# A decoder block in fp32r: where the attention matrices are transposed, when the cross-attention steps run, a second buffer for Wq's rows, and every second place for the ternary pieces

## The chip, the core and the metric

The kernel runs on one core of one Trainium2 chip. The metric is device time in microseconds (us), lower is better. All times below are of the same inputs.

## What is computed

x and ctx have shape 4 x 512 x 512. Three residual blocks follow each other, each behind a layer norm (LN, eps 1e-5):

```
x = x + attn(LN(x))          # 16 heads of 128; q, k, v = LN(x) @ W + b; softmax; @ Wo + bo
x = x + gamma * xattn(LN(x), ctx)   # 8 heads of 64, softmax over 512, along the sequence axis
x = x + ffn(LN(x))           # silu(x @ w1q.T) * (x @ w3q.T) @ w2q.T, hidden 1365
# w1q, w3q, w2q: ternary: s = mean|w|; clip(round(w / s), -1, 1) * s
```

The attention of a head attends over the 128 features and not over the sequence (q is transposed to 128 x 512, k to 512 x 128), so a score matrix is 128 x 128 per head and batch, and it can be had from the Gram matrix G = LN(x)^T LN(x) of a batch.

## The kernel before, in words

All products are made of fp32r pieces: an operand is split into a rounded high part (made by ScalarE, ACT) and the rest (made by VectorE, DVE, or GpSimd, POOL), and `three_passes` (L131 to L133) issues three matmuls for each product: high x high, low x high, high x low.

The four batches are worked in two passes p of two batches i (PB = 2). The 16 heads are in four groups. In a pass:

- *Gram*: G of each batch, four tiles of 12 matmuls.
- *Scores*, for each group g: eight M tiles M(c, i) = G Wk, c = 0..3 ("places" 0 to 7), 12 matmuls each; behind places 3, 5 and 7 the steps `pe_s`, which multiply M with Wq's rows into two score banks (banks 4 and 5). ACT takes the exponentials (`act_attention_half`), TensorE (PE) transposes the results T(g, pr) (pr = 0, 1), ACT copies them to `ptf`.
- *Values*, for each group j: four Y tiles of batch 0, eight R tiles, four Y tiles of batch 1, and then out tiles: four of batch 0 and four of batch 1, 12 matmuls each, into banks 6 and 7 in turn. DVE adds each into `xacc` (`dve_out`, L1699); an out tile waits for the addition of the tile two before it (`out_free`).

The G, M, Y and R tiles go through a ring of four PSUM banks, 0 to 3 (`attention_tiles`, `attention_banks`): a bank is free when DVE has made the low part out of it (`a_free`). The order in the ring is worked out ahead, by the list that `attention_tiles` yields.

**Ternary pieces and the next pass's layer norm** run on DVE in pass 0's values (`dve_between`). There are SLOTS = 15 places in each group j: one behind each of the four Y tiles of batch 1, behind each of the eight out tiles, and behind the first three Y tiles of the group that follows. With k = 15 j + n, of three places two take one of 24 ternary pieces (L1777 and L1779, 105 x 832 elements each), and the third takes one of 14 parts of the layer norm of batches 2 and 3: parts 0 and 1 are two statistics each, part 2 is the long one (four L1534, a copy L1535, and `newton_rsqrt`, 12 small instructions on 128 x 4 elements, L120 to L126, each of which waits for the one before it), parts 3 to 6 normalise a row block each.

**The cross-attention of batch 0** is put into pass 1's scores, in steps n = 0..31 (h = n // 4, q = n % 4). A step is on PE: in the middle of an M tile the four transposes of an earlier head's quarter (`pe_pt`, L471, into bank 7), behind the tile the two score matmuls (`pe_sx`, L481 and L482, into bank 6), and in some steps eight `pe_ret` matmuls (L493, L494, into bank 3). Other engines: DVE maximum L692, ACT exponential L604, POOL scaling L845, ACT `act_px` and DVE `dve_px` (L687), which splits the transposed quarter and frees bank 7. Banks 6 and 7 are one buffer each here (ring=1), and bank 3 is lent to `pe_ret`, so the ring of M tiles has three banks. `early_step(g, place)` says which step a place has: nine steps in each group (a ninth, "place 8", behind place 5), and step 0 at place 4 of group 0. Bank 7 also takes the transposes T(g-1, 0) (behind place 3) and T(g-1, 1) (behind place 6), L1134, and the transposes of ctx's values V (`pe_vt`, L459), once in eight steps.

Before each group's M tiles DVE and POOL add a row (bias and first row of the weight) to Wk's and Wq's rows. Both rows go through one buffer `rowb`: SyncE (SP) loads Wk's row, DVE uses it; then SP loads Wq's row, DVE prepares it at place 7 ahead of its part of the split of Wk (`dve_split_a`, L1585), and POOL adds it.

SP issues all loads and stores from one queue in the order of the code, and a wait in it holds up everything behind it. In pass 1's scores that queue holds, among others, the store of x1 and of its statistics, and the loads of each head's rows (`sp_head`), each of which waits for the head two before it.

**The statistics of x1** (the first block's result), `dve_x1`, have four parts: two statistics each in parts 0 and 1, the means and the Newton chain in part 2, and the store in part 3. For batch 0 of a pass a part stands ahead of each of the last four out tiles; for batch 1 of pass 0 behind places 0 to 3 of the next scores; for batch 1 of pass 1 behind steps 0 to 3 of the first turn of what follows.

After pass 1 come four turns, each with the cross-attention of a batch beside the feed-forward of the one before it. Batch 0's layer norm ahead of the feed-forward, `dve_x3`, stands ahead of the last eight out tiles of pass 1.

## Time and profile before

| | us |
|---|---|
| median of three runs | 1197.58 (1197.43 to 1199.67) |
| the profiled execution, its own time | 1199.98 |
| its span | 1198.2 |
| PE busy | 1128.2 (94%) |
| DVE busy | 753.8 (63%) |
| ACT busy | 553.0 (46%) |
| POOL busy | 464.1 (39%) |

The profile's first part gives each engine's busy time. Its views used below are: who waited for whom on an engine, with the sum, the count and the longest; the windows, that is the busy time of each engine in a stretch with its count of instructions, and PEclk, the granted clock as a share of full speed; the timeline of an engine; and the chain of waits, the work that ended last, followed back. The times are from the span's start. The stages in this execution: pass 0's scores end near 170 us, its values at 391.9, pass 1's scores near 571, its values near 783, and the four turns fill the rest.

### The profile page before, as it was taken

What the parts mean: (1) busy time and instruction counts of PE and PEld (TensorE: products, weight loads), DVE (VectorE), ACT (ScalarE), POOL (GpSimd) and SP (SyncE); (2) the same over time, 40 slices, a digit from 0 to 9 for tenths busy, and PEclk for the clock granted to TensorE, in tenths of its full rate; (3) what the DMA queues carried; (4) which work ended last, traced back from release to release, by engine and by line L of the source; (5) the groups of instructions that cost most, each with busy time, mean ns of one, the idle gap of its engine ahead of it and who ended that gap; (6) DMA issues with size and microseconds to landing.
All of it is one profiled execution on the core that took longest, in us unless ns stands there. A gap on an engine that the chain in (4) does not pass through costs nothing.

```text
span 1198.2 us, 15780 instructions
## 1 busy us (share of the span) xinstructions
PE 1128.2 (94%) x5792; PEld 941.3 (79%) x5792; DVE 753.8 (63%) x1389; ACT 553.0 (46%) x1145; POOL 464.1 (39%) x400
## 2 busy tenths in 40 slices
PE   4999998899999898989999999989999999999997
PEld 4888886778788777778788888768877888888776
DVE  7555459797566676675523244688857876787431
ACT  2455672223242265555633252167627762875230
POOL 2222328141432165554271340046626651764030
PEclk9999999999999999999999999999999999999999
DMA  6465654455301832321440203272104111310000
GB/s 228 129 178 177 210 176 129 164 156 196 111 7 47 228 115 71 111 75 45 156 184 1 71 3 138 69 220 72 50 27 122 55 45 50 110 44 2 36 1 35
DMA packets 53846, 121.13 MB, mean 101 GB/s; under 512 B 10009, under 2 KB 10009, under 8 KB 51722
## 3 DMA queue, kind: packets, MB, share of 16 engines
q1 hardware_dynamic: 53770, 120.13, 31.6%
q8 instruction: 46, 0.75, 0.3%
q14 instruction: 30, 0.25, 0.1%
HBM read 102.27 MB, written 17.84 MB: 100 GB/s over the span
## 4 chain that ended last, share of the span: by engine, by line
PE 77%; DVE 10%; ACT 5%; issue 3%; DMA 1%; POOL 1%; SPq 1%; POOLq 0%; DVEq 0%; ACTq 0%
PE bank L131 15%; PE bank L132 15%; PE bank L133 15%; PE bank L508 6%; PE bank L509 6%; PE bank L471 4%; PE bank L522 3%; PE bank L523 3%; PE bank L493 2%; PE bank L494 2%; PE bank L481 2%; PE bank L482 2%; DVE wlow L1777 1%; DVE xmx L692 1%; POOL wal L1825 1%
## 5 line engine op out<-in xcount | busy, mean ns | idle before, releaser
L508 PE MATMUL bank<-x3h,w 128*128 128x512 f32 (+1 forms) x352 | 141.7, 403 | 1.9 <-DVE x3l L765 1.7
L1310 ACT ACTIVATE yh<-bank 128x512 fp32r<-128x512 f32 x64 | 38.1, 600 | 222.5 <-PE bank L133 222.4
L509 PE MATMUL bank<-x3l,w 128*128 128x512 f32 (+1 forms) x352 | 138.8, 394 | 0.0
L131 PE MATMUL bank<-yh,rh 128*128 128x512 f32 x256 | 102.6, 401 | 12.6 <-DVE xacc L1699 12.6
L131 PE MATMUL bank<-wah,gh 128*128 128x512 f32 x256 | 105.1, 411 | 5.6 <-DVE wal L1585 4.6
L1825 POOL TENSOR_TENSOR wal<-raw_a,wah 128x512 fp32r<-128x512 f32 x44 | 63.1, 1462 | 116.7 <-ACT wah L1332 116.7
L845 POOL TENSOR_SCALAR pe_x<-pe_x,xri,gam 128x512 f32<-128x512 f32 x96 | 76.3, 795 | 81.4 <-DVE xri L696 77.4
L692 DVE TENSOR_REDUCE xmx<-bank 128x1 f32<-128x512 f32 x128 | 87.5, 684 | 31.2 <-PE bank L482 30.4
L1552 DVE TENSOR_TENSOR yl<-bank,yh 128x512 fp32r<-128x512 f32 x64 | 44.1, 691 | 99.1 <-ACT yh L1310 99.1
L131 PE MATMUL bank<-wah,ph 128*128 128x512 f32 x256 | 100.4, 392 | 0.3 <-POOL wal L1825 0.3
L132 PE MATMUL bank<-yl,rh 128*128 128x512 f32 x256 | 100.7, 393 | 0.0
L133 PE MATMUL bank<-wah,gl 128*128 128x512 f32 x256 | 100.7, 393 | 0.0
L133 PE MATMUL bank<-yh,rl 128*128 128x512 f32 x256 | 100.7, 393 | 0.0
L132 PE MATMUL bank<-wal,gh 128*128 128x512 f32 x256 | 100.5, 393 | 0.0
L1830 POOL TENSOR_TENSOR wbl<-raw_b,wbh 128x512 fp32r<-128x512 f32 x64 | 87.4, 1392 | 32.1 <-ACT wbh L1352 31.8
L132 PE MATMUL bank<-wal,ph 128*128 128x512 f32 x256 | 99.8, 390 | 0.0
L133 PE MATMUL bank<-wah,pl 128*128 128x512 f32 x256 | 99.7, 389 | 0.0
L1699 DVE SCALAR_TENSOR_TENSOR xacc<-bank,rinv,xacc 128x512 f32<-128x512 f32 x64 | 47.9, 749 | 65.7 <-PE bank L133 65.3
L852 POOL TENSOR_TENSOR gtl<-gf,gth 128x512 fp32r<-128x512 f32 (+1 forms) x44 | 56.8, 1291 | 57.8 <-ACT gth L621 57.3
L508 PEld LDWEIGHTS bank<-x3h,w 128*128 128x128 f32 (+1 forms) x352 | 65.2, 185 | 16.9 <-issue 2.5
L604 ACT ACTIVATE pe_x<-bank,xmx 128x512 f32<-128x512 f32 x96 | 66.0, 688 | 25.9 <-DVE xmx L692 25.0
L1552 DVE TENSOR_TENSOR ml<-bank,mh 128x512 fp32r<-128x512 f32 x64 | 43.6, 687 | 53.3 <-ACT mh L1310 53.2
(167 smaller groups left out, 3033.4 us busy)
## 6 DMA issues: line engine op xcount, KB each, us to landing
raw_a<-in_wk SPq DMA_DIRECT2D x8, 1024.0 KB, 5.3
raw_b<-in_wq SPq DMA_DIRECT2D x8, 1024.0 KB, 5.5
raw_a<-in_wo SPq DMA_DIRECT2D x8, 1024.0 KB, 5.3
raw_b<-in_wvt SPq DMA_DIRECT2D x8, 1024.0 KB, 4.9
ternary_scratch<-wraw SPq DMA_DIRECT2D x24, 341.2 KB, 3.0
x1d<-x_scratch SPq DMA_DIRECT2D x48, 128.0 KB, 3.0
kd<-in_ctx SPq DMA_DIRECT2D x48, 128.0 KB, 3.1
w<-ternary_scratch SPq DMA_DIRECT2D x2, 2730.0 KB, 10.9
```

The lines of the kernel that those rows point to most:

```text
L131: pe.matmul(out, wh, xh, start=start, stop=False, skip_group_check=shared)
L132: pe.matmul(out, wh, xl, start=False, stop=False, skip_group_check=shared)
L133: return pe.matmul(out, wl, xh, start=False, stop=stop, skip_group_check=shared)
L508: pe.matmul(u_bank[w][0:m, :], lhs, x3h[:, c, :], start=c == 0, stop=False)
L509: mm = pe.matmul(u_bank[w][0:m, :], lhs, x3l[:, c, :], start=False, stop=c == CK - 1)
L604: act.activation(m.pe_x[:, q, :], m.s[q % 2][:], ACT.Exp, bias=xmx[:, q:q + 1], accum_out=xrs[:, q:q + 1]).then_inc(s["s_free"], 1)
L692: dve.reduce_max(xmx[:, q:q + 1], m.s[q % 2][:], axis=AX, negate=True).then_inc(s["xmx"], 1)
L845: pool.tensor_scalar(m.pe_x[:, q, :], m.pe_x[:, q, :], xri[:, q:q + 1], gam[:], ALU.mult, ALU.mult).then_inc(s["xpn"], 1)
L852: pool.tensor_tensor(gtl[0:m, i, :], gf[0:m, :], gth[0:m, i, :].bitcast(F32), ALU.subtract).then_inc(s["gl2"], 1)
L1552: dve.tensor_tensor(dst, a_bank(u)[:], high.bitcast(F32), ALU.subtract).then_inc(s["a_free"], 1)
L1825: pool.tensor_tensor(wal[:, c, :], raw_a[:, c, :], wah[:, c, :].bitcast(F32), ALU.subtract).then_inc(s["wal_pool"], 1)
L1830: pool.tensor_tensor(wbl[:, c, :], raw_b[:, c, :], wbh[:, c, :].bitcast(F32), ALU.subtract).then_inc(s["wbl"], 1)
```

## The change

Five edits go together. `T_PAIR` and `split` only keep the counts of `a_free` and `a_hi` right, since the T tiles take a place in the ring but are freed by another semaphore.

1. *Ring.* In pass 1 T and V are tiles of the ring (three banks), no longer in bank 7. T(g-1, 0) stays behind place 3, V(g) stands behind place 5's `pe_s`, T(g-1, 1) between `pe_s(g, 2)` and `pe_s(g, 3)` at the group's end. The transposes of the step at place 0 of the next group go to the group's end too, ahead of `pe_s(g, 3)`.
2. *Steps.* Groups have 6, 9, 9 and 8 steps; step 0 is at place 2 of group 0. The head's first loads and x1's store are issued at the end of pass 0's values, and the first head's operands are made at place 0.
3. *Wq's row* has a buffer `rowq`; DVE prepares it behind the maxima of the group's end.
4. *Ternary pieces* in every second place, 24 pieces in places k = 0, 2, ..., 46; the layer norm's parts in the odd places k = 13 to 39.
5. *x1's statistics*: one of each row block right behind its `dve_out`; the rest in two parts, ahead of the last four out tiles for batch 0, at places 0 and 1 for batch 1 of pass 0, and behind steps 6 and 10 of the first turn for batch 1 of pass 1. `dve_x3` goes behind the first out tile. SP's store of the last statistics goes behind the loads of the turn.

```diff
 def ternary_steps(j):
-    return [k // 3 * 2 + k % 3 for k in range(max(0, SLOTS * j - CK + 1), SLOTS * j + 3 * CK) if k % 3 < 2 and k // 3 * 2 < TERNARY]
+    return [k // 2 for k in range(max(0, SLOTS * j - CK + 1), SLOTS * j + 3 * CK) if k % 2 == 0 and k // 2 < TERNARY]
...
+                if p == PASSES - 1 and c == 1 and g:
+                    yield "T", g - 1, 0
+                if p == PASSES - 1 and c == 2:
+                    yield "V", g
+            if p == PASSES - 1 and g:
+                yield "T", g - 1, 1
...
+FIRST_STEP = (-2, 6, 15, 24)
 def early_step(g, place):
-    n = len(PLACES) * g - 4 + PLACES.index(place)
+    order = PLACES if g in (1, 2) else range(2 * CK)
+    if place not in order:
+        return None
+    n = FIRST_STEP[g] + order.index(place)
     return n if n >= 0 else None
...
+        rowq = put("rowq", 152 * KB, [P, 2, 512])
...
         def pe_scores_early(pe):
...
                     if place == 3:
                         pe_s(pe, p, g, 0)
                         if g:
-                            pe_t_early(pe, g - 1, 0, tiles_before(early_step(g, 4)))
+                            pe_t_early(pe, g - 1, 0)
                     if place == 5:
                         pe_s(pe, p, g, 1)
-                        pe_early_turn(pe, early_step(g, 8))
-                        pe_early_scores(pe, early_step(g, 8))
-                    if place == 6 and g:
-                        pe_t_early(pe, g - 1, 1, tiles_before(early_step(g, 7)))
-                    if place == 7:
-                        pe_s(pe, p, g, 2)
-                        pe_s(pe, p, g, 3)
+                        pe_v_early(pe, g)
+                        if early_step(g, 8) is not None:
+                            pe_early_turn(pe, early_step(g, 8))
+                            pe_early_scores(pe, early_step(g, 8))
+                pe_s(pe, p, g, 2)
+                if g:
+                    pe_t_early(pe, g - 1, 1)
+                if g + 1 < GROUPS:
+                    pe_early_turn(pe, early_step(g + 1, 0))
+                pe_s(pe, p, g, 3)
...
         def dve_scores_early(dve, link):
...
-                        if place == 2 * CK - 1:
-                            dve_row(dve, link, p, g + 1, "b")
-                            dve.sem_inc(s["row_sum"], 1)
...
                 dve_split_a(dve, p, g + 1)
...
+                    dve_early_rows(dve, early_step(g + 1, 0))
...
                 dve_maxima(dve, p, g)
+                if g + 1 < GROUPS:
+                    dve_row_q(dve, g + 1)
...
         def dve_between(dve, link, p, j, n):
...
                 k = SLOTS * j + n
-                if k // 3 * 2 < TERNARY and k % 3 < 2:
-                    dve_ternary(dve, k // 3 * 2 + k % 3)
-                elif k // 3 * 2 < TERNARY:
-                    dve_normalise(dve, link, p + 1, k // 3 // LN_PARTS, k // 3 % LN_PARTS)
-                elif k - TERNARY < PB * LN_PARTS:
-                    dve_normalise(dve, link, p + 1, (k - TERNARY) // LN_PARTS, (k - TERNARY) % LN_PARTS)
+                part = (k - 1) // 2 - SLOTS // 2 + 1
+                if k % 2 == 0 and k // 2 < TERNARY:
+                    dve_ternary(dve, k // 2)
+                elif k % 2 and 0 <= part < PB * LN_PARTS:
+                    dve_normalise(dve, link, p + 1, part // LN_PARTS, part % LN_PARTS)
...
                 for a in range(HG):
                     dve_out(dve, p, j, 0, a)
+                    if last:
+                        dve_x1_tile(dve, link, p, 0, a)
                     dve_between(dve, link, p, j, CK + a)
-                    if last and not further:
-                        dve_x3n(dve, 0, a)
+                    if last and not further and a == 0:
+                        dve_x3(dve, 0, [0])
+                    elif last and not further:
+                        dve_x3n(dve, 0, a - 1)
+                if last:
+                    dve_x1(dve, link, p, 0, 0)
+                    dve_x1(dve, link, p, 0, 1)
...
-                if n < 4:
-                    dve_x1(dve, link, PASSES - 1, 1, n)
+                if n in (6, 10):
+                    dve_x1(dve, link, PASSES - 1, 1, n == 10)
```

The new order of SP's queue in pass 1's scores, written out:

```diff
+            sp_x1_data(sp, p - 1, 1)
+            sp_slot_a(sp, p, 1)
+            sp_row_k(sp, p, 1)
+            sp_slot_b(sp, p, 1)
+            sp_row_q(sp, p, 1)
+            sp_head(sp, early, 0, 2)
+            sp_x1_stat(sp, p - 1, 1)
+            sp_head(sp, early, 0, 3)
+            sp_values_early(sp, 2)
+            sp_slot_a(sp, p, 2)
+            sp_row_k(sp, p, 2)
+            sp_head(sp, early, 0, 4)
+            sp_row_q(sp, p, 2)
+            sp_head(sp, early, 0, 5)
+            sp_slot_b(sp, p, 2)
+            sp_values_early(sp, 4)
...
```

## Rows read from the trace of the kernel before

**Rows 1.** The page: the engines' busy time, share of the span, and instructions.
```profile
PE 1128.2 (94%) x5792; PEld 941.3 (79%) x5792; DVE 753.8 (63%) x1389; ACT 553.0 (46%) x1145; POOL 464.1 (39%) x400
```

**Rows 2.** Who waited for whom on PE, whole span: us, times, longest.
```profile
PE bank L131 <- DVE wal L1585: 4.6, 7, 0.9
PE bank L481 <- POOL e_qst L839: 4.1, 1, 4.1
PE bank L459 <- DVE e_pxl L687: 2.9, 3, 2.0
...
PE bank L471 <- ACT ptf L1358: 2.8, 3, 1.3
...
PE bank L471 <- DVE e_pxl L687: 1.4, 1, 1.4
...
PE bank L481 <- ACT e_pe_x L604: 1.3, 3, 0.6
```

**Rows 3.** Windows: stretch, us, busy per engine (instructions), PEclk, DMA share, GB/s.
```profile
185.45:218.34 32.89, 24.76 (x98) 18.73 (x96) 30.88 (x40) 7.21 (x13) 25.92 (x17) 0.95 0.36 109
245.88:269.14 23.26, 22.34 (x97) 17.87 (x96) 22.11 (x24) 7.21 (x13) 13.62 (x8) 1.00 0.49 153
380.99:391.87 10.88, 10.88 (x49) 9.01 (x48) 8.56 (x27) 0.60 (x1) 0.00 (x0) 1.00 0.01 2
393.00:434.00 41.00, 35.32 (x173) 29.16 (x172) 26.25 (x57) 16.08 (x37) 12.39 (x11) 0.96 0.68 193
434.00:592.00 158.00, 144.56 (x827) 121.97 (x826) 102.01 (x174) 93.28 (x227) 83.73 (x75) 0.99 0.27 87
755.38:785.00 29.62, 26.98 (x121) 21.56 (x119) 21.94 (x60) 4.57 (x8) 2.57 (x2) 0.94 0.09 36
```

**Rows 4.** Timeline of DVE in the first group's out tiles: start, us, work.
```profile
190.75 0.74 DVE L1699 SCALAR_TENSOR_TENSOR xacc<-bank,rinv,xacc 128x512 f32<-128x512 f32 x1
...
197.15 2.50 DVE L1777 TENSOR_SCALAR wlow<-wraw,wthr 105x832 f32<-105x832 f32 x1
...
207.74 1.21 DVE L120 TENSOR_SCALAR nvar<-nvar 128x4 f32<-128x4 f32 x1
```

**Rows 5.** Timeline of DVE in the second group, and at its end.
```profile
239.16 0.64 DVE L1777 TENSOR_SCALAR wlow<-wraw,wthr 105x832 f32<-105x832 f32 x1
239.84 1.09 DVE L1779 SCALAR_TENSOR_TENSOR wraw<-wraw,wthr,wlow 105x832 f32<-105x832 f32 x1
...
243.99 0.69 DVE L1552 TENSOR_TENSOR yl<-bank,yh 128x512 fp32r<-128x512 f32 x1 [0.35 <-ACT yh L1310]
...
249.06 2.00 DVE L1779 SCALAR_TENSOR_TENSOR wraw<-wraw,wthr,wlow 105x832 f32<-105x832 f32 x1
...
278.13 0.69 DVE L1552 TENSOR_TENSOR yl<-bank,yh 128x512 fp32r<-128x512 f32 x1 [0.35 <-ACT yh L1310]
...
282.19 0.69 DVE L1552 TENSOR_TENSOR yl<-bank,yh 128x512 fp32r<-128x512 f32 x1
```

**Rows 6.** Timeline of POOL in the second group.
```profile
247.27 6.55 POOL L1825 TENSOR_TENSOR wal<-raw_a,wah 128x512 fp32r<-128x512 f32 x4 [8.08 <-ACT wah L1332]
```

**Rows 7.** The chain of waits in pass 1's scores: start, us, what.
```profile
400.62 6.98 DMA e_kd<-in_ctx
...
424.94 3.48 DMA rowb<-in_wq
```

**Rows 8.** Who waited for whom on PE from 755 to 810 us.
```profile
PE bank L481 <- ACT pe_x L604: 4.4, 3, 1.7
PE bank L131 <- DVE xacc L1699: 2.6, 1, 2.6
```

**Rows 9.** Timeline of DVE in the first turn: x1's part 2, and the maximum behind it.
```profile
791.40 0.81 DVE L1534 BATCH_NORM_AGGREGATE mvar<-bst 128x2 f32<-128x6 f32 x4
...
794.90 0.69 DVE L692 TENSOR_REDUCE xmx<-bank 128x1 f32<-128x512 f32 x1
```

**Rows 10.** The page's last part: DMA issues, count, KB each, us to landing.
```profile
raw_b<-in_wq SPq DMA_DIRECT2D x8, 1024.0 KB, 5.5
```

More of the change, by code:

```diff
@@ L103, with split @@
 A_BANK = attention_banks()
+T_PAIR = {u: ((PASSES - 1) * GROUPS + key[1]) * 2 + key[2] for key, u in A.items() if key[0] == "T"}
+def split(u):
+    return u + 1 - sum(v <= u for v in T_PAIR)
 Mem = namedtuple("Mem", "x1d kd vd qst kh kl vts pe_x pxh pxl x2 s t r ring")
 PLACES = (0, 1, 2, 3, 4, 5, 8, 6, 7)
+FIRST_STEP = (-2, 6, 15, 24)
 def early_step(g, place):
-    n = len(PLACES) * g - 4 + PLACES.index(place)
+    order = PLACES if g in (1, 2) else range(2 * CK)
+    if place not in order:
+        return None
+    n = FIRST_STEP[g] + order.index(place)
     return n if n >= 0 else None
@@ L348, in x3_bank @@
         def x3_bank(b, t):
-            return bank[4 + t % 2] if b == 0 else main.t[t_x3(0, t) % 2]
+            return bank[4 + t % 2] if b == 0 else main.t[t_x3(b, t) % 2]
         def turns(body):
@@ L1059, in pe_bank @@
             where, before = A_BANK[u]
-            if before is not None:
-                pe.wait_ge(s["a_free"], before + 1)
+            if before in T_PAIR:
+                pe.wait_ge(s["att_free"], T_PAIR[before] + 1)
+            elif before is not None:
+                pe.wait_ge(s["a_free"], split(before))
                 if where == RING_A - 1 and before < A["M", PASSES - 1, 0, 0, 0] < u:
@@ L1121, in pe_t @@
                     pe.wait_ge(s["t_free"], t_p(0, XH - 1, 3) + 1)
-                if n >= 2:
+                if n >= 2 and not p:
                     pe.wait_ge(s["att_free"], n - 1)
@@ L1126, in pe_t, with pe_t_early, pe_v_early @@
                 mm.then_inc(s["att_ready"], 1)
-        def pe_t_early(pe, g, pr, before):
-            p = PASSES - 1
-            pe.wait_ge(s["s_read"], pair(p, g, pr) + 1)
-            pe.wait_ge(s["t_free"], before)
+        def pe_t_early(pe, g, pr):
+            u = A["T", g, pr]
+            pe.wait_ge(s["s_read"], pair(PASSES - 1, g, pr) + 1)
+            pe_bank(pe, u)
             for q in range(4):
-                mm = pe.transpose(early.t[0][:, q * P:(q + 1) * P], pw[:, pr, q * P:(q + 1) * P], ident[:])
-            mm.then_inc(s["att_ready"], 1)
+                mm = pe.transpose(a_bank(u)[:, q * P:(q + 1) * P], pw[:, pr, q * P:(q + 1) * P], ident[:])
+            mm.then_inc(s["a_ready"], 1)
+        def pe_v_early(pe, g):
+            u = A["V", g]
+            pe.wait_ge(s["vd_in"], 16 * (g + 1))
+            pe_bank(pe, u)
+            for c in range(CK):
+                mm = pe.transpose(a_bank(u)[:, c * P:(c + 1) * P], early.vd[:, c * P:(c + 1) * P], ident[:])
+            mm.then_inc(s["a_ready"], 1)
         def pe_early_scores(pe, n):
@@ L1168, in pe_scores_early @@
                     pe_m_tile(pe, p, g, c, i, range(0, CK // 2))
-                    if n is not None:
-                        if g and place == 4:
-                            pe.wait_ge(s["att_free"], pair(p, g - 1, 0) + 1)
-                        if g and place == 7:
-                            pe.wait_ge(s["att_free"], pair(p, g - 1, 1) + 1)
+                    if n is not None and (place or g == 0):
                         pe_early_turn(pe, n)
@@ L1419, in act_scores_early @@
                     c, i = divmod(place, PB)
-                    if early_step(g, place) is not None:
-                        act_early_rows(act, early_step(g, place))
+                    n = early_step(g, place)
+                    if n is not None and (place or g == 0):
+                        act_early_rows(act, n)
                     act_high(act, mh[:, c % 2, i, :], A["M", p, g, c, i])
@@ L1629, in dve_early_max, with dve_v_early @@
             dve_max(dve, early, 0, h, q)
+        def dve_v_early(dve, g):
+            tb, high, low = v_tile_early(g)
+            dve.wait_ge(s["a_hi"], split(A["V", g]))
+            dve.tensor_tensor(low, tb, high.bitcast(F32), ALU.subtract).then_inc(s["a_free"], 1)
         def dve_early_values(dve, n):
             h, q = divmod(n, 4)
-            if n == 0:
-                dve_vt(dve, early, 0, 0)
-            elif n % 8 == 7 and h + 1 < XH:
-                dve_vt(dve, early, 0, h + 1)
             if q == 0 and h + 1 < XH:
@@ L1651, in dve_scores_early @@
                         dve_early_values(dve, n)
[L1652 removed]
+                    if g == 0 and place == 0:
+                        dve_q(dve, early, 0, 0)
+                    if g == 0 and place < 2:
                         dve_x1(dve, link, p - 1, 1, place)
[L1654 to L1655 removed]
                     if place == 1 and g:
@@ L1867, in pool_scores_early @@
                         pool_matrix(pool, p, 0)
-                    if place == 5:
+                    if place == 5 and early_step(g, 8) is not None:
                         pool_early(pool, early_step(g, 8) - 1)
```

213 lines of the change are left out of this document (119 added, 94 removed), and 1 row of the table s.

## The prediction, written before the result was known

> **What bounds the kernel now.** I read the page first: PE is busy 1128.2 of a span of 1198.2 us, the other engines at most 63% [rows 1]. So TensorE is the bound, no instruction is taken away from it by the change (T, V and the steps' transposes are moved, not dropped), and all that can be won is in the 70 us in which PE is idle and in the stretches where it runs slowly. The windows come next [rows 3]; they show where the idle time lies. A tile of 12 matmuls costs 10.88 / 4 = 2.72 us when nothing disturbs it (48 instructions, 380.99 to 391.87). The eight out tiles of pass 0's first group need 21.76 us by that and take 32.89: 11.1 us lost, of which 8.1 is idle and the rest a lowered clock (PEclk 0.95 of 32.89 us is 3.3 us at the lower of the two levels, 1.2 GHz, which costs 1.6) and slow first matmuls behind a wait. The second group's take 23.26, 1.5 lost; the third repeats it. Pass 1's scores with the cross steps: 41.00 - 35.32 = 5.7 idle and 158.00 - 144.56 = 13.4 idle, together 19.1, and PEclk 0.96 and 0.99 give another 1.6 + 1.6 = 3.2. The end of pass 1's values: 2.6 idle and 0.06 x 29.62 = 1.8 of clock. Then PE's waits [rows 2, 8] name who is late in each: in the values DVE's addition L1699, in the scores half a dozen causes of 1 to 4 us each. The other waits of PE (the start, the later turns, the end) are not touched by the change, and I leave them alone.
>
> **Ternary pieces, first group.** A piece is 0.64 + 1.09 = 1.73 us when POOL is quiet [rows 5]. Beside POOL its two instructions take up to 2.50 [rows 4] and 2.00 [rows 5]. Before, two pieces follow each other behind two out tiles: 2 x (2.50 + 2.00) + 2 x 0.74 for the additions [rows 4] is over the 5.44 us that PE needs for two tiles, with only two banks of slack. The long part of the layer norm also falls there, with small instructions on 128 x 4 elements at 1.2 us each (L120 stands for four of them) [rows 4]. Afterwards two tiles carry one piece, at most 4.5 + 1.5 = 6.0, and about 1.0 + 2.0 + 1.5 = 4.5 where no piece meets a long POOL instruction, and no layer norm part before k = 13. I put the rest at 0.5 of 11.1: 10.6 gained.
>
> **Second group: the long part meets POOL's split.** It is now at k = 17, behind the third Y tile of batch 1, with pieces at k = 16 and 18. Before, from the start of such a low part (278.13) to the start of the one behind the long part (282.19) it is 4.06 us [rows 5], that is 3.4 us for 17 small instructions, 0.20 each. Set behind the low part at 243.99 it ends at 248.05. But at 247.27 POOL begins its four splits of 6.55 us together [rows 6], which are followed by four more. 0.78 us are left then, four instructions, and they are of the kind with two inputs in SBUF. The trace has none of these small ones beside POOL, so bounds: 0.20 each, as alone, or one POOL instruction of 1.2 to 1.6 us each, like the small L120 [rows 4] and as 6.55 / 4. The large two-input instruction L1779 goes from 1.09 to 2.00 beside POOL [rows 5], so I take the upper bound, nearest in kind: with some 1.3 each behind 247.27 less the first, which may slip in, the chain ends near 252.0, then low part 0.7, piece at k = 18 3.0, addition 0.75: 256.5. PE wants that addition at 245.88 + 2 x 2.72 = 251.3. Stall 5.2, and as it is as long as those that lowered the clock [rows 3], 1.7 more: 6.9 against 1.5 now, a loss of 5.4. With the lower bound the chain ends at 248.05, the addition at 253.2, stall 1.9: a loss of 0.4.
>
> The Trainium skill, page "SBUF — State Buffer", section "Who interferes with whom", says that VectorE and GpSimd share one pair of SBUF ports under an exclusive lock, which a VectorE instruction needs when it has two SBUF inputs, so that the one that comes second waits for the whole instruction of the other. L1779 and L120 agree; by that rule the four are held and the stall is the long one, while without it this edit is nearly free. No row here decides it.
>
> **Third group.** The long part of the other batch is at k = 31, behind the second Y tile, and ends 2 us before POOL starts. Two pieces no longer meet: 1.5 falls to 0.3, and 0.6 that the long part cost at the end of the second group goes: 1.8 gained. In the last group the last piece (k = 46) delays SP's load of the next Wk by some 40 us. DVE needs it behind the last Y tile; a load of this size takes 5.5 us [rows 10], from a piece that ends some 4 us before that: 1 to 2 us late on DVE, and PE has four Gram tiles (10.9 us) there as cover: nothing. Sum for pass 0's values: 10.6 - 5.4 + 1.8 = 7.0 (12.0 with the lower bound).
>
> **The scores with the cross steps: 22.3 us (19.1 idle, 3.2 clock) to be had.** Step by step from PE's waits [rows 2]:
> - e_qst, 4.1 and its 1.6 of clock. PE waits for the first head's operands, whose loads are issued 9 us behind pass 0's last addition and land 6.98 us later [rows 7]. In the change x1's statistics are ready some 15 us earlier (one per tile, the Newton chain while PE has Gram tiles, POOL quiet), so SP issues the loads before the scores begin, and ACT and POOL have places 0 to 2 (8.2 us) for their copies and splits, two instructions each, even against a first step two places earlier. Gone; if the cover failed, it would be the 4.1 again. SP's new order puts 12 DMA issues of 0.6 ahead of x1's second store; that store is needed only much later.
> - The bank of V and T: 2.9 (V behind `dve_px`), 2.8 (the steps' transposes behind ACT's copy of T), and the second 1.6 of clock, which I put down to the longest V wait (2.0). In the ring each holds a bank that PE wants again three tiles later, at least 5.4 us on; ACT's copy is 0.6. Gone. The price of what comes in its place is bounded by the same rows: at worst 2.8 again, now on an M tile; below nothing it can't be. I take 0.3.
> - wal, 4.1 of the 4.6 in this stage: at a group's end PE waits for DVE's split, which stands behind Wq's row, and this once behind its load of 3.48 us [rows 7]. In the change the row goes behind the maxima, and PE has T and a step's transposes (2 x 0.44) more before it needs the split. In return `pe_s(g, 3)` and the exponentials come 0.9 later, `dve_px` stands ahead of the maxima, and POOL's additions to raw_b start some 3 us later; ACT splits raw_b only two places on, which hides that. I leave 1.2 of 4.1.
> - ACT's exponentials, 1.3: its work at a group's end grows by T's copy and a px, and I leave 0.8.
> - e_pxl 1.4 behind the last steps, in an order that nothing changes, stays.
> - The rest of the 22.3 (22.3 - 5.7 - 7.3 - 4.1 - 1.3 - 1.4 = 2.5, single waits of about 1 us for other low parts), of which I leave 2.3.
> Left: 0.3 + 1.2 + 0.8 + 1.4 + 2.3 = 6.0, gained 16.3. The first group's 11.1 hold 11.1 - 8.1 - 1.6 = 1.4 of slow first matmuls behind five waits; a dozen waits less give 0.7 here at a quarter of that price: 17. Bounds: 8 (see the rivals) and 22.
>
> **The end of pass 1's values.** Before, `dve_x3` stands ahead of the first addition: 2.6 of wait [rows 8] and 1.8 of clock [rows 3]. Afterwards it stands behind it (3.7 us; the second addition is then 0.8 late), and x1's chain of some 4 us ahead of the last four additions (0.9 late). 4.4 becomes 1.7: 2.7 gained; bounds 0 and 4.4.
>
> **The first turn.** x1's parts stretch DVE there: the part from 791.40 to the maximum at 794.90 is 3.5 us [rows 9], and PE waits 4.4 for exponentials [rows 8]. The change has 1 us of it behind step 6 and a chain of 13 small instructions behind step 10. There POOL is busy about half of the time, so the chain takes between 2.6 and, held as above, 6 us, on a DVE with about 1.4 us to spare in a step. I take 3.0 of new wait: 1.4 gained; bounds -1.6 and 4.
>
> **Sum.** 7.0 + 17 + 2.7 + 1.4 = 28.1 off the profiled execution's 1199.98 (its span 1198.2 and 1.8 around it), which is 2.4 above the median of 1197.58. Taken off the median: 1169.5; I say 1170.
>
> **Rivals.**
> - *The small instructions are not held by POOL.* Then pass 0's values give 12.0 and the turn 2.9: 6.5 more, 1163. For it: no small two-input instruction is seen held. Against it: L1779 is.
> - *The waits of the scores move instead of going.* Each cause there sits within 1 us of the next (ACT, DVE and POOL all have work for some 60% of this stage), so when PE comes sooner, the exponentials at a group's start and `dve_px` are late next. Half of the 17 is given back: 1178 to 1179. For it: the waits are spread over six causes. Against it: DVE is busy only 102.01 of 158.00 us there [rows 3].
> - *Most of it goes:* the small instructions are free (6.5) and the scores keep 2 us instead of 6 (4 more): 1159. For it only that the cover in each step looks longer than I price it.
> - *Slower: SP's queue.* The load of Wq for the next group now stands behind two heads' loads and behind Wq's row, which waits for POOL's additions, which wait for DVE's row behind the maxima. If that chain delivers raw_b later than the group's end, all of PE's next `pe_s` waits. A load takes 5.5 us [rows 10], and it is wanted at the end of a group of about 45 us, so the room is over 10 us in each of three groups. It decides from there: the change is slower than before only if each group is late by over 9.4 us beyond that room (3 x 9.4 = 28.1). Then it is 1198 to 1205.
> - *It doesn't do what it says*: no stall goes, since the waits named are not the true ones: 1197 to 1199. The clock dips and waits sit at the same places, so I see little for it.
>
> **Chances.** Forecast (1164 to 1175) 0.47; not held (1160 to 1165) 0.2; waits moved (1175 to 1186) 0.2; most of it goes (1153 to 1160) 0.07; slower 0.04; no change 0.02. The likeliest one's price is 1170. For the range I take 1155 to 1184: it leaves out some 0.08 at the far end of the moved waits, the slower case, no change, and the tip of the case where most goes. A difference under 0.2% (2.4 us) can't be told from none here: faster 0.94, same 0.02, slower 0.04.
>
> **What the changed kernel's profile would show.** The first group's out tiles in 22 to 23 us. In the second group's, a wait for L1699 of about 5 us behind four small L124 to L126 of over 1 us each; if these take 0.16 each, the first rival holds. No wait of L481 for e_qst and no lowered clock near 411 us; no wait of L459, nor of L471 for ptf. In the windows of pass 1's scores 5 to 8 us of idle PE instead of 19.1; if it is 12, the second rival holds, and the names of the waits tell where they went. One or two short waits for L1699 near the end of pass 1. A wait of L481 for pe_x near step 12 of the first turn. The forecast is wrong if the scores' idle doesn't fall by over 8 us.

## The result

The changed kernel takes 1170.58 us (median of four runs, 1168.34 to 1170.99) against 1197.51 (1196.81 to 1199.67) for the kernel before on the same chip: ratio 0.9768, 95% interval 0.9751 to 0.9786, so 27 us or 2.3% faster. The forecast was 1170. Its profiled execution takes 1170.35 us, with a span of 1168.6 and a mean granted clock of 0.997 (before 1199.98, 1198.2 and 0.992): 29.6 us less.

The first row of the changed kernel's page answers to [rows 1]: PE is busy 9.3 us less with the same 5792 matmuls. In part that is because fewer of them run at the lower clock (granted clock 0.992 before, 0.997 now).

```profile
PE 1118.9 (96%) x5792; PEld 938.8 (80%) x5792; DVE 743.5 (64%) x1389; ACT 551.6 (47%) x1145; POOL 461.0 (39%) x400
```

The windows of the changed kernel, with columns as in [rows 3], follow. The first three are the eight out tiles of pass 0's first, second and third group, then pass 1's scores with the early Y tiles, then the end of pass 1's values. The row under them is the kernel before, for the same work as the fourth.

```profile
184.92:206.68 21.76, 21.76 (x98) 18.02 (x96) 16.99 (x17) 7.21 (x13) 21.76 (x14) 1.00 0.42 128
234.22:261.83 27.61, 23.59 (x97) 19.06 (x96) 22.31 (x35) 7.21 (x13) 11.65 (x8) 0.94 0.36 108
289.37:311.13 21.76, 21.76 (x97) 18.02 (x96) 19.56 (x27) 7.21 (x13) 13.17 (x8) 1.00 0.42 129
382.89:562.25 179.36, 173.66 (x993) 148.79 (x992) 123.74 (x228) 108.63 (x261) 95.36 (x85) 1.00 0.34 106
726.88:752.62 25.74, 24.17 (x114) 19.46 (x112) 22.50 (x61) 3.54 (x6) 2.58 (x2) 1.00 0.11 42
```

```profile
391.87:590.75 198.88, 179.76 (x993) 150.82 (x992) 129.01 (x231) 109.10 (x261) 96.13 (x85) 0.98 0.36 108
```

A table by stage, from the starts of the first matmul of each in the two profiled executions:

| stage | before | after | gained | forecast |
|---|---|---|---|---|
| to the first matmul | 15.26 | 14.74 | 0.5 | 0 |
| pass 0's values, whole | 235.92 | 227.46 | 8.5 | 7.0 |
| - first group's out tiles | 32.89 | 21.76 | 11.1 | 10.6 |
| - second group's | 23.26 | 27.61 | -4.4 | -5.4 |
| - the rest of the third group's term | | | 2.4 | 1.8 |
| pass 1's scores and cross steps | 198.88 | 179.36 | 19.5 | 17 |
| end of pass 1's values | 28.01 | 25.74 | 2.3 | 2.7 |
| first turn to the end | 414.81 | 415.94 | -1.1 | 1.4 |

Besides, 0.7 is lost in pass 0's last group, at a single gap at 355.5 us. It comes from the late load of the next Wk's row. DVE waits 6.2 us for that row, which lands at 346.33, and its first addition of the group starts 5.2 us behind the group's first out tile instead of 3.2. The kernel before with the fourth edit alone has the same wait of 6.2 and the same gap (at 357.24), so the gap comes with that edit.

What PE waited for in pass 1's scores with the early Y tiles, after the change, columns as in [rows 2]:

```profile
PE bank L501 <- DVE e_pxl L717: 1.4, 1, 1.4
PE bank L511 <- ACT e_pe_x L634: 1.3, 1, 1.3
PE bank L150 <- DVE e_x L737: 1.1, 1, 1.1
PE bank L150 <- DVE wal L1655: 0.7, 1, 0.7
PE bank L150 <- DVE ml L1615: 0.6, 1, 0.6
PE bank L150 <- POOL wal L1917: 0.5, 2, 0.3
```

The waits for e_qst (4.1), for V's bank (2.9) and for ACT's copy of T (2.8) of [rows 2] are gone. The timelines of DVE and POOL in the second group, where time was lost (start, us, work), answer to [rows 5, 6]:

```profile
235.59 0.16 DVE L145 SCALAR_TENSOR_TENSOR rstd<-ntmp,rstd 128x4 f32<-128x4 f32 x1
235.79 1.16 DVE L143 TENSOR_TENSOR ntmp<-rstd 128x4 f32<-128x4 f32 x1
236.98 1.22 DVE L144 SCALAR_TENSOR_TENSOR ntmp<-ntmp,nvar 128x4 f32<-128x4 f32 x1
238.23 1.22 DVE L145 SCALAR_TENSOR_TENSOR rstd<-ntmp,rstd 128x4 f32<-128x4 f32 x1
239.49 0.69 DVE L1615 TENSOR_TENSOR yl<-bank,yh 128x512 fp32r<-128x512 f32 x1
240.09 1.03 DVE L1864 TENSOR_SCALAR wlow<-wraw,wthr 105x832 f32<-105x832 f32 x1
241.16 1.97 DVE L1866 SCALAR_TENSOR_TENSOR wraw<-wraw,wthr,wlow 105x832 f32<-105x832 f32 x1
```

```profile
235.61 5.05 POOL L1917 TENSOR_TENSOR wal<-raw_a,wah 128x512 fp32r<-128x512 f32 x4 [8.09 <-ACT wah L1378]
```

POOL's splits begin at 235.61. The small instruction that starts 0.18 later takes 1.16 us instead of 0.16, and the two behind it take 1.22 each: about as long as one of POOL's instructions (5.05 / 4 = 1.26).

### The profile page after: what moved, and what is told of

It is laid out like the page before. It is cut to its first block, busy times and chain, and to the rows that moved or that the text cites. A ratio compares the mean times of both kernels' runs of the same rounds, so it can differ in the third digit from the quotient of the medians.

```text
span 1168.6 us, 15784 instructions
## 1 busy us (share of the span) xinstructions
PE 1118.9 (96%) x5792; PEld 938.8 (80%) x5792; DVE 743.5 (64%) x1389; ACT 551.6 (47%) x1145; POOL 461.0 (39%) x400
## 4 chain that ended last, share of the span: by engine, by line
PE 83%; DVE 7%; ACT 4%; issue 2%; POOL 2%; DMA 1%; SPq 0%; POOLq 0%; DVEq 0%; ACTq 0%
PE bank L150 17%; PE bank L151 17%; PE bank L152 17%; PE bank L538 6%; PE bank L539 6%; PE bank L501 4%; PE bank L552 4%; PE bank L553 4%; PE bank L523 2%; PE bank L524 2%; PE bank L511 2%; PE bank L512 2%; POOL wal L1917 1%; DMA kd<-in_ctx 1%; ACT wah L1378 1%
## 5 line engine op out<-in xcount | busy, mean ns | idle before, releaser
L1917 POOL TENSOR_TENSOR wal<-raw_a,wah 128x512 fp32r<-128x512 f32 x44 | 59.7, 1382 | 117.2 <-ACT wah L1378 117.2
L1779 DVE SCALAR_TENSOR_TENSOR xacc<-bank,rinv,xacc 128x512 f32<-128x512 f32 x64 | 47.9, 749 | 64.1 <-PE bank L152 63.0
L634 ACT ACTIVATE pe_x<-bank,xmx 128x512 f32<-128x512 f32 x96 | 65.9, 687 | 26.9 <-DVE xmx L722 26.1
L865 POOL TENSOR_TENSOR kl<-kd,kh 128x512 fp32r<-128x512 f32 x24 | 31.0, 1292 | 119.5 <-ACT kh L613 119.5
```

Of the source, the lines that this page charges most:

```text
L634: act.activation(m.pe_x[:, q, :], m.s[q % 2][:], ACT.Exp, bias=xmx[:, q:q + 1], accum_out=xrs[:, q:q + 1]).then_inc(s["s_free"], 1)
L1779: dve.scalar_tensor_tensor(xacc[:, i, a, :], late_bank(n)[:], rinv[:, j, a // 2, q:q + 1], xacc[:, i, a, :], ALU.mult, ALU.add).then_inc(s ...
L1917: pool.tensor_tensor(wal[:, c, :], raw_a[:, c, :], wah[:, c, :].bitcast(F32), ALU.subtract).then_inc(s["wal_pool"], 1)
```

## Experiments

Each experiment is one edit of the changed kernel, unless it says otherwise. Ratios are to the kernel before on the same chip; in those terms the changed kernel is 0.9768. Stage lengths are read like those of the table; of kernels whose edit doesn't touch a stage they repeat within some 0.1 us (pass 1's scores to the first Y tile: 159.60 to 159.62 in eight of them), but from the first turn on they differ by up to 3 us, so there only the starts of the first turn's steps are compared.

**POOL begins its splits only when the long part is through.**

```diff
+                    if part == 2:
+                        dve.sem_inc(s["ln_long"], 1)
...
                     pool_matrix(pool, p, j + 1)
+                    if p == 0 and j == 1:
+                        pool.wait_ge(s["ln_long"], 1)
                     pool_split_a(pool, p, GROUPS + j + 1)
```

> The changed kernel with one wait more, on POOL: in pass 0's second group of the values it begins its four splits of Wv only when DVE's long layer norm part is through. DVE's order is the changed kernel's. Theory (POOL's instructions hold DVE's small ones): POOL is about 1 us later, no small instruction lasts over 0.3 us, the eight out tiles of the second group take 21.8 to 23 us instead of 27.61, no wait of 4 us for DVE's addition, and the time falls by 5 to 6 us to about 1165. Rival (DVE simply has too much work in those places, with or without POOL): the tiles stay at 26 us or more and the time at 1169 to 1171. Third possibility: the split comes late and PE waits for it at the next group's start; then the gain shows in the out tiles and is lost behind them, and the wait names POOL's or DVE's split.

Measured: 1166.34 us, ratio 0.9723 (0.9701 to 0.9746). The window of the second group's out tiles, and DVE at the chain's end, with all nine two-input instructions of the chain at 0.16 (the last is shown):

```profile
234.35:257.56 23.21, 22.05 (x97) 17.95 (x96) 20.54 (x35) 7.21 (x13) 13.02 (x8) 1.00 0.43 128
...
236.32 0.16 DVE L145 SCALAR_TENSOR_TENSOR rstd<-ntmp,rstd 128x4 f32<-128x4 f32 x1
236.63 0.69 DVE L1615 TENSOR_TENSOR yl<-bank,yh 128x512 fp32r<-128x512 f32 x1
237.24 1.13 DVE L1866 TENSOR_SCALAR wlow<-wraw,wthr 105x832 f32<-105x832 f32 x1
```

That is 4.4 us less in this stage, with DVE's order unchanged and POOL 1 us later: the hold is the cause, not the amount of work on DVE.

**Batch 2's layer norm one odd place earlier.**

```diff
-                part = (k - 1) // 2 - SLOTS // 2 + 1
+                part = (k - 11) // 2 if k < 25 else (k - 13) // 2 if k > 25 else -1
```

> The changed kernel with batch 2's seven layer norm parts each one odd place earlier (k = 11 to 23 instead of 13 to 25), so that the long one stands at k = 15, behind the first Y tile of batch 1 and not the third. No wait is added; POOL is as before. Theory (held by POOL): the long part ends some 2 us before POOL's splits begin; out tiles of the second group 21.8 to 23 us, time about 1165. Rival (too much work on DVE): the same pieces, parts and additions stand there, only their order differs, so at most half of the 4.35 lost there comes back: 1168 to 1169.

Measured: 1166.42 us, ratio 0.9720 (0.9698 to 0.9742). The window of the same tiles is:

```profile
234.57:256.93 22.36, 22.06 (x98) 17.95 (x96) 19.05 (x24) 7.21 (x13) 13.06 (x8) 1.00 0.49 147
```

That is 5.2 less, more than half of the loss and more than with POOL's wait, which still left 1.45 above the undisturbed 21.76. The rival falls.

**The fourth edit alone, on the kernel before.**

```diff
+    return [k // 2 for k in range(...) if k % 2 == 0 and k // 2 < TERNARY]
...
+                part = (k - 1) // 2 - SLOTS // 2 + 1
+                if k % 2 == 0 and k // 2 < TERNARY:
+                    dve_ternary(dve, k // 2)
+                elif k % 2 and 0 <= part < PB * LN_PARTS:
```

> The kernel before with the fourth edit alone: ternary pieces in every second place, the layer norm's parts in the odd places 13 to 39. Theory (the edits act in stages of their own and add up): first group's out tiles near 21.8 us (before 32.89), the second's near 27.6 (23.26), the third's 21.8 (23.26), scores of pass 1 unchanged at about 179; together 8 to 9.5 us less than before, 1188 to 1190. Rival (part of the gain needs the other edits, or is given back in pass 1's start, where POOL and DVE would now be the later ones): under 6 us less.

Measured: 1191.17 us, ratio 0.9927 (0.9904 to 0.9949), that is between 8 and 9 us less. The out tiles of the three groups take 21.76, 28.80 and 21.76, and pass 0's values as a whole 228.66 (7.3 less). Pass 1's scores with the steps take 177.62 to the first Y tile, against 179.13 before and 159.60 in the changed kernel. The 1.5 less was not expected there; it shows as shorter waits for e_qst (3.4 instead of 4.1) and for DVE's split (3.3 instead of 4.1), and why they are shorter isn't shown. So the edits nearly act in stages of their own: at most 1.5 of the 19.5 can be from this one.

**V in bank 7 again.**

```diff
-                if p == PASSES - 1 and c == 2:
-                    yield "V", g
...
-            u = A["V", g]
-            pe.wait_ge(s["vd_in"], 16 * (g + 1))
-            pe_bank(pe, u)
...
+            pe_vt(pe, early, 0, 2 * g)
```

> The changed kernel with V's four transposes in bank 7 again, the bank of the steps' transposes, at the same places of PE's order; T stays in the ring. Theory (the bank of V and T was one cause): PE waits again at V for DVE's split of the step before, and at the step behind V for V's own: 2 to 3 us more idle in pass 1's scores, with a clock dip of 1.6 if one wait is over 2 us, so 1172.5 to 1175. Rival (the new step places and the row's place did it, the bank hardly matters): under 1 us more, 1170 to 1171.5.

Measured: 1175.88 us, ratio 0.9803 (0.9781 to 0.9824). To the first Y tile it is 163.99 us instead of 159.60, 4.4 more. The wait is the one expected, of the steps' transposes for DVE's split of V (the first line; 3.6 us):

```profile
PE bank L504 <- DVE e_vts L1705: 3.6, 2, 2.1
PE bank L514 <- ACT e_pe_x L637: 1.3, 1, 1.3
PE bank L151 <- DVE wal L1653: 0.7, 1, 0.7
```

The bank of V is worth more here than the 2 to 3 us expected. Only V was moved; T alone wasn't tried.

**Late start of the first heads' loads.**

```diff
                 sp_row(sp, wq, bq, 0)
-                sp_early_start(sp)
...
             sp_row_k(sp, p, 1)
+            sp_early_start(sp)
             sp_slot_b(sp, p, 1)
```

> The changed kernel, but SyncE issues batch 0's x1 store, the statistics' loads and the first two heads' loads where they stood before: in the scores, behind the loads of Wk and of its row. The steps keep their new places (step 0 at place 2). Theory (the early start is what took away the wait for the first head's operands): PE waits 4.1 us plus up to the 5.4 us by which step 0 is two places earlier, and the clock falls once: 6 to 11 us more than the changed kernel, 1176 to 1182, all of it before 20 us behind the first M tile. Rival (x1's statistics, which come 15 us earlier in any case, let the queue get there in time): under 2 us more.

Measured: 1185.85 us, ratio 0.9895 (0.9878 to 0.9911). Up to the first Y tile it takes 16.1 us more, 15.2 of it in one wait. SyncE's queue (start, us of each issue), here and then in the changed kernel, shows why it is more than the 11 expected:

```profile
PE bank L511 <- POOL e_qst L869: 15.2, 1, 15.2
...
387.16 0.50 SPq L948 DMA_DIRECT2D stat_scratch<-stat  x1
396.29 1.35 SPq L411 DMA_DIRECT2D stx<-stat_scratch  x2
```

```profile
366.77 0.33 SPq L948 DMA_DIRECT2D stat_scratch<-stat  x1
368.25 1.35 SPq L411 DMA_DIRECT2D stx<-stat_scratch  x2
```

The queue stands until x1 and its statistics are stored (x1 is 1 MB, issued 0.7 ahead of them): 9.1 us here and 1.5 in the changed kernel, where x1's store was issued 4.6 ahead. The edit also does more than was expected of it, so it overstates what the early start is worth. In the kernel before, x1's store of batch 0 was not behind the loads of Wk and its row: it was issued at 371.09, 21 us ahead of the first M tile, and the statistics' loads followed 4.1 us behind the start of that tile. Here they follow 13.8 behind it. Without those 9.1 us of standing, 7 of the 16.1 would be left, an estimate that lies in the 6 to 11 expected. The theory's wait is there, and the rival (under 2 us) falls, but its size against the kernel before wasn't measured.

**Wq's row ahead of DVE's split.**

```diff
+                if g + 1 < GROUPS:
+                    dve_row_q(dve, g + 1)
                 dve_split_a(dve, p, g + 1)
...
                 dve_maxima(dve, p, g)
-                if g + 1 < GROUPS:
-                    dve_row_q(dve, g + 1)
```

> The changed kernel, but DVE prepares Wq's row ahead of its split of Wk again, not behind the maxima. The row's own buffer and its early load stay. Theory (the row's place on DVE delayed the split): PE waits for DVE's split at three groups' ends, 0.5 to 1 us each beyond the 0.7 of the changed kernel: 1.5 to 3 us more, 1172 to 1173.5. Rival (only the load of the row through one buffer made that wait): under 0.5 us more.

Measured: 1174.91 us (1170.86 to 1175.23), ratio 0.9791 (0.9774 to 0.9808), too wide to tell by itself. The stage tells: it takes 161.63 us to the first Y tile, 2.0 more, and PE's wait for the split is 2.7 instead of 0.7, as expected:

```profile
PE bank L150 <- DVE wal L1655: 2.7, 3, 1.5
```

**The same steps per group as before.**

```diff
-FIRST_STEP = (-2, 6, 15, 24)
+FIRST_STEP = (-4, 5, 14, 23)
...
-    order = PLACES if g in (1, 2) else range(2 * CK)
+    order = PLACES
```

> The changed kernel with 4, 9, 9 and 9 plus one steps as before (step 0 at place 4 of the first group, a ninth step behind place 5 in every group), instead of 6, 9, 9 and 8. Ring, early loads and Wq's row as changed. Theory (the ring, the early loads and the row's place made the gain; how many steps a group has hardly matters): within 1 us of the changed kernel, 1169.5 to 1171.5. Rival (a ninth step at place 5 of the last group and the step's turn at each group's end need the new dealing): 2 to 5 us more, 1172.5 to 1175.5, as waits for e_pxl and the maxima in the last group.

Measured: 1170.27 us, ratio 0.9762 (0.9735 to 0.9789). It takes 158.50 us to the first Y tile, 1.1 less than the changed kernel; PE's wait for the exponentials at a step is 0.2 instead of 1.3, and the 0.7 for DVE's split is gone. The new dealing gained nothing: it cost 1.1, and the other edits made the gain.

The rest is about the first turn. The table gives the start of a step's first score matmul, counted from step 0's, in us. The column "six like it" gives the range of the six kernels with the changed kernel's turn: POOL's wait, the earlier layer norm, V, the late start, the row and the steps. They show how far the same code varies. Between steps 13 and 14 the clock falls in them (PEclk 0.96 over the turn's first 48 us in the one with the row), and in the changed kernel's profiled execution it doesn't (1.00). It also falls there with x2 and w2 later, and between steps 11 and 12 with the chain spread; with w2 alone later, with the chain in the tail and in all three it doesn't fall.

| step | before | changed | six like it | x2, w2 later | w2 later | spread | tail | all three |
|---|---|---|---|---|---|---|---|---|
| 7 | 18.24 | 14.20 | 14.20-14.21 | 14.19 | 14.20 | 14.20 | 14.20 | 14.20 |
| 11 | 29.90 | 27.41 | 26.80-27.56 | 25.84 | 25.86 | 26.80 | 26.77 | 25.85 |
| 12 | 33.63 | 31.84 | 31.23-31.95 | 29.58 | 29.59 | 34.22 | 31.20 | 29.58 |
| 13 | 34.45 | 35.51 | 34.70-35.65 | 32.47 | 32.73 | 35.14 | 32.02 | 30.40 |
| 16 | 44.69 | 45.78 | 46.51-47.23 | 44.29 | 43.03 | 47.15 | 42.26 | 40.64 |

**Head 3's loads ahead of x2's and w2's.**

```diff
             sp_head(sp, main, 1, 2)
-            sp_w2(sp)
+            sp_head(sp, main, 1, 3)
             sp.wait_ge(s["x2_kept"], TJ)
             sp.dma_start(main.x2[:], x1_dram[1]...).then_inc(s["x2_in"], 16)
+            sp_w2(sp)
-            for h in range(3, XH):
+            for h in range(4, XH):
```

> The changed kernel, but in the first turn SyncE issues head 3's loads ahead of x2's load (1 MB) and of w2's (2.8 MB), and w2's behind x2's. Theory (head 3's loads land late, at about 777, since they share the DMA engines with the two large ones): head 3's waits (ACT's kh, PE's 1.6 and 0.5 near 780) go, 2 us less, 1168.5. Rival (the loads' delay is hidden and the gaps at 780 are DVE's and ACT's load): within 0.5 us of the changed kernel. Against both: x2 comes later, and dve_ret of head 0 may wait for it; then about 1 us is lost near step 10.

Measured: 1166.75 us, ratio 0.9732 (0.9717 to 0.9746). In the changed kernel the chain of waits shows the load of 128 KB that holds head 3, and then DVE's long chain. ACT's wait for that load is the last line:

```profile
764.52 13.13 DMA kd<-in_ctx
777.65 0.02 issue
777.67 0.63 ACT kh L613
...
782.79 0.62 DVE nvar L139
783.41 0.02 issue
783.44 0.73 DVE ntmp L140
...
ACT kh L613 <- DMA kd<-in_ctx: 4.0, 1, 4.0
```

With the loads ahead step 11 is 1.6 us earlier and step 12 2.3 (against the best of the six, 1.0 and 1.7), and ACT no longer waits for head 3's data: the theory holds.

**w2's load alone behind head 3's.**

```diff
             sp_head(sp, main, 1, 2)
-            sp_w2(sp)
...
             for h in range(3, XH):
                 sp_head(sp, main, 1, h)
+                if h == 3:
+                    sp_w2(sp)
```

> The changed kernel, but w2's load (2.8 MB) is issued behind head 3's loads; x2's load (1 MB) stays ahead of them. It tells which of the two large loads head 3's data wait for. If it is w2's: head 3's data land before 772, the wait near 780 goes, as in the kernel with both behind: 1.5 to 2.3 us less, 1168.5. If it is x2's, just ahead in the queue: they land at about 777 still or a little earlier, within 0.5 us of the changed kernel.

Measured: 1168.08 us (1166.62 to 1170.40), ratio 0.9748 (0.9717 to 0.9778); steps 11 and 12 come as early as with both behind. Head 3's four loads land in the changed kernel, and here (issues, KB each, median us to landing):

```profile
x1d<-x_scratch SPq DMA_DIRECT2D x2, 128.0 KB, 12.4
kd<-in_ctx SPq DMA_DIRECT2D x2, 128.0 KB, 12.4
```

```profile
x1d<-x_scratch SPq DMA_DIRECT2D x2, 128.0 KB, 5.6
kd<-in_ctx SPq DMA_DIRECT2D x2, 128.0 KB, 5.0
```

x2's 1 MB stood ahead of them in both, so it is w2's 2.7 MB, issued 4.4 us before head 3's first load, that delayed them by 7 us.

The kernel before had nearly the same landing. Counted from step 0, w2's load is issued at 6.0 us there and at 5.6 in the changed kernel. Head 3's first load is issued at 14.2 and 10.0, and its last one lands at 24.3 and 25.0. The steps are what moved: ACT came to these data at 24.8 in the kernel before, without a wait, and is ready for them at 21.1 now.

**x1's chain spread over six steps.**

```diff
-                if n in (6, 10):
-                    dve_x1(dve, link, PASSES - 1, 1, n == 10)
+                if n in X1_STEPS:          # (5, 6, 9, 11, 13, 15)
+                    dve_x1_piece(dve, link, PASSES - 1, 1, X1_STEPS.index(n))
```

> The changed kernel, but the Newton chain of x1's statistics in the first turn does not stand in one piece behind step 10: means behind step 5, then pieces of three small instructions (the last of two) behind steps 6, 9, 11, 13 and 15. Theory (13 small instructions in a row make the exponentials of the steps behind late, 2.8 us near 788): that gap goes and no piece makes one of its own, 2 to 3 us less, 1168. Rival (each piece meets POOL and is held, or the gap is from another cause): within 0.5 us of the changed kernel.

Measured: 1172.10 us, ratio 0.9775 (0.9761 to 0.9790). The theory fell. Step 12 is 2.3 to 3.0 us later than in all others with the load's delay, where part of it is the clock, which falls just ahead of this step here (PEclk 0.51 from 783.60 to 787.10). Steps 13 and 16 are where they were. The wait is another: for DVE's addition of a step's result to x2, 0.3 us in the changed kernel.

```profile
PE bank L524 <- DVE x L738: 3.0, 2, 1.9
```

The rival named for it shows too: in three of the pieces' instructions DVE is held, for 1.11, 0.97 and 1.15 us, where in the one long piece it is held twice, for 0.69 and 0.72. So cutting the chain up doesn't help. Whether unheld pieces would have isn't shown.

**x1's chain in the turn's tail.**

```diff
+            tail(0)
             if f is not None:
                 dve_y(dve, f, 0)
...
                 dve_x3l(dve, b, 1)
+            tail(1)
...
             for b in range(2, B):
                 sp_rows(sp, b, b - 2)
+                if b == 2:
+                    sp_x1_stat(sp, p, 1)
```

> The changed kernel, but x1's means and Newton chain are taken out of the first turn's steps and put into its tail, where DVE has idle time: the means behind the last preparation of the next turn's first head, the chain behind the second x3l. SyncE's store of these statistics goes behind the next batch's loads. Theory (in steps 6 to 20 DVE is busy without a gap, so that anything in them, in one piece or spread, comes late at PE): the 3.5 us lost at steps 12 and 13 against the kernel before go; the wait for head 3's data (1.6) stays: 2 to 3.5 us less than the changed kernel, 1167.5. Rival (the steps are late from DMA and POOL, whatever DVE does): within 0.7 us. If the tail has no room, the wait shows there as L489 for x3l.

Measured: 1167.32 us (1165.72 to 1170.07), ratio 0.9738 (0.9711 to 0.9764). Step 13 is 2.7 us earlier than in the best of the six and step 16 is 3.5 earlier than in the changed kernel (4.3 earlier than in the best of the six, whose clock falls), while step 11 keeps its delay by the load. The theory holds.

**All three: earlier layer norm, loads ahead, chain in the tail.**

> The changed kernel with batch 2's layer norm parts one odd place earlier, with head 3's loads ahead of x2's and w2's in the first turn, and with x1's chain in the turn's tail. Theory: the three act in different places or on different causes and nearly add up: 5.2 (measured on the second group's out tiles) + 1.8 to 2.3 + 2 to 3.5 = 9 to 11 us less than the changed kernel, 1160 to 1162. Rival (in the first turn the two edits remove the same wait, since steps 11 to 13 wait for whichever is last): 7 to 8 us less, 1163.

Measured: 1160.56 us (1160.40 to 1161.01), ratio 0.9679 (0.9657 to 0.9702): 10.0 us below the changed kernel's median (10.7 by the ratios) and the fastest of all. The second group's tiles take 22.36 us, steps 13 and 16 come 5.1 earlier, and the mean granted clock is 0.999. The total is in the 9 to 11 expected. In the turn the parts overlap some: at step 13 the loads alone give 3.0 and the tail alone 3.5, 6.5 together, against 5.1.

## Why the prediction was right, and where it was off

- *First group, 10.6 against 11.1.* The tiles now take 21.76, exactly the undisturbed 8 x 2.72, although POOL is busy all the time in this window. The forecast left 0.5 that isn't there. The fourth edit alone shows the same 21.76.
- *Second group, -5.4 against -4.4.* The mechanism is as written, and the two experiments on it show it: small instructions on 128 x 4 elements are held by POOL's instruction. Three were held, not four: the chain of 17 had got one further when POOL began, 3.28 us behind the low part's start by the forecast and as measured. The forecast's own terms, one that slips in and three of 1.3, end the chain at 251.4 and not at 252.0; in the same way the addition of its lower bound ends at 252.5 and not at 253.2. The stall was 4.0 (forecast 5.2), with one fall of the clock (PEclk 0.94). Here the Trainium skill, page "SBUF — State Buffer", section "Who interferes with whom", says that a VectorE instruction with two SBUF inputs contends with a GpSimd one that reads SBUF, under an exclusive lock. The trace agrees, and shows that this holds for 128 x 4 elements too (1.16 to 1.22 us). L120, which the forecast named for the rule, has only one SBUF input and does not bear on that case.
- *Third group, 1.8 against 2.4; last group 0 against -0.7.* The forecast had the cause in the last group, the next Wk's load behind the last ternary piece, and its size on DVE (1 to 2 us late; the addition comes 2.0 later). What it had wrong is the cover: it put the effect on PE at nothing, because PE has four Gram tiles there, and 0.7 came through.
- *Pass 1's scores, 17 against 19.5.* The sum of the waits is right nearly to the tenth: the forecast left 6.0 of idle PE, and it is 179.36 - 173.66 = 5.7. The term that was mis-sized is PE's busy time beyond the clock, which the forecast put down to slow first matmuls. PE's busy time for the same 993 matmuls fell from 179.76 to 173.66, 6.1; 3.2 of it is the two falls of the clock by [rows 3], and 2.9 the rest, for which the forecast had 0.7. PE starts again behind 20 gaps of over 0.1 us before and behind 7 after. A first matmul of 512 columns takes 0.31 to 0.34 us there to the next one's start, where others take 0.23. With the smaller ones that makes about 0.8 of the 2.9; what the other 2.1 are isn't shown. By single edits undone in the changed kernel, V's bank is worth 4.4, the row's place 2.0 and the new dealing itself -1.1. The late start costs 16.1, of which some 9 come from where that edit put x1's store. These need not add up to 19.5, and T's bank was never measured alone.
- *End of pass 1's values, 2.7 against 2.3.* There are two waits for L1779 of 0.8 us, where 0.8 and 0.9 were forecast, and no fall of the clock.
- *First turn, +1.4 against -1.1.* This is the step that failed. Its first half was right: with x1's parts out of steps 0 to 3, step 7 comes 4.0 us earlier (4.4 of waits in [rows 8]). The chain behind step 10 costs 3.5 at step 13 (forecast 3.0; only 2.1 where head 3's data come early). What the forecast left out is what waits behind a gain: it let the 4.4 through to the later steps but for the chain. Head 3's data, behind w2's load, land 24.3 us behind step 0 before and 25.0 after, and steps that come 4 us earlier run into them. That costs 1.0 to 1.6 us at step 11 and 0.7 more at step 12. Moving the statistics' store let head 3's loads be issued 4.1 us earlier, and they land no earlier for it, since w2's load is still under way. With both removed (all three) step 16 comes 5.1 earlier, that is 4.05 ahead of the kernel before, and all of the gain of step 7 is kept.
- *Rivals.* "Not held by POOL" is out by experiment. "The waits move" is out in the scores, where 5.7 us of idle time are left, but in the first turn it is what happened. "Most of it goes" is out: the small instructions were held, and 5.7 us stayed. SP's queue was late nowhere in the scores.

That the total of 1170 was met within 0.6 us is partly luck: 2.5 us more than forecast were gained in the scores and 1.5 more in pass 0's values, and 2.5 less from the first turn on. The stages add up to 29.7 us in the profiled executions, 1.6 more than the 28.1 of the sum, while the medians differ by 26.9, since the profiled execution before was 2.5 us above its median.

## What to carry to other kernels

A chain of small dependent VectorE instructions is cheap (0.2 us each) only where GpSimd is quiet; place it by GpSimd's timeline, or let GpSimd wait 1 us for it. When steps are made to come earlier, look at what they will run into next: which data they need, when these land now, and which large transfer is still under way ahead of them. Issuing a small load earlier in a queue doesn't help if that large one stays ahead of it. When PE has many short waits, removing them can give back more than the waits: here 6.1 us of busy time for 13.4 of idle time, 3.2 of it from the clock and about 0.8 from first matmuls.

## What the runs showed of the hardware

- In a chain of small dependent DVE instructions, one was held per instruction of POOL, until that one ended (1.16 to 1.22 us instead of 0.16). In the kernel before, one-input ones were held too (L120 1.21 us, [rows 4]), and so were L139 and L140 in the first turn of the changed kernel (0.62 and 0.73 us in the chain of waits).
- Loads of 128 KB that are issued 4.4 us behind one of 2.7 MB land after 12.4 us, and after 5.0 to 5.6 when it is behind them. With the load of 1 MB behind them as well, steps 11 and 12 come no earlier (25.84 and 29.58 against 25.86 and 29.59).
- A wait of PE of 4.0 us was followed by the lower clock (0.94 in that window); the wait of 2.6 us ahead of step 13 of the first turn was followed by it in one kernel (0.96, with the row ahead) and not in the changed kernel (1.00).
